# A five-layer-step graph network on one core: the late scatters go from a straight line of 196 into a loop that first copies each round

## The reference

```python
h = jnp.maximum(_layernorm(x, axis=-1), 0.0)
x = x + _L0_gnn_ref(...)   # relu(segment_sum(h[src] @ w[edge_type], dst) + h @ w_loop + b)
h = jnp.maximum(_layernorm(x, axis=-1), 0.0)
x = x + _L1_gnn_ref(...)   # attention with 4 heads over the edges, segment_sum over src
h = jnp.maximum(_layernorm(x, axis=-1), 0.0)
x = x + _L2_gnn_ref(...)   # two steps of: x @ W_self.T + mean_of_neighbours @ W_neigh.T + b, layer norm
h = jnp.maximum(_layernorm(x, axis=-1), 0.0)
x = x + _L3_gnn_ref(...)   # segment_sum((h @ W)[src] * norm, dst)
```

## Time and profile before

| | busy us (share of the span) | instructions |
|---|---|---|
| PE | 2799.7 (58%) | 19724 |
| DVE | 2506.3 (52%) | 11513 |
| ACT | 1947.0 (40%) | 5394 |
| POOL | 2441.8 (50%) | 2379 |

### The profile page before, as it was taken

How to read it: one execution, slowest core, us unless ns; L and a number is a source line. 1 busy time by engine, 2 the same in 40 slices (tenths; PEclk the granted TensorE clock), 3 DMA queues, 4 the chain that set the end, 5 groups by cost and what they waited for, 6 DMA issues and landing times.

```text
span 4854.1 us, 81538 instructions
## 1 busy us (share of the span) xinstructions
PE 2799.7 (58%) x19724; PEld 2445.3 (50%) x19724; DVE 2506.3 (52%) x11513; ACT 1947.0 (40%) x5394; POOL 2441.8 (50%) x2379
## 2 busy tenths in 40 slices
PE   6888877774665630067710675665128857751288
PEld 5887876654555520056610454565016646640277
DVE  5666668874555448823300784332019964430298
ACT  2222236664444421145500683232016645530187
POOL 5556635667888854455577003555740025557400
PEclk9999999997777765578855897887559978875599
DMA  4444437872333349811121783111129951111288
GB/s 153 158 156 160 158 125 240 240 220 46 41 41 41 41 101 309 278 40 38 42 64 60 238 282 113 36 35 52 55 85 321 318 162 39 37 57 55 91 278 262
DMA packets 328251, 638.77 MB, mean 132 GB/s; under 512 B 61072, under 2 KB 89776, under 8 KB 321992
## 3 DMA queue, kind: packets, MB, share of 16 engines
q1 hardware_dynamic: 233406, 501.99, 31.7%
q0 software_dynamic: 90944, 133.85, 12.5%
q10 hardware_dynamic: 3786, 1.65, 0.1%
HBM read 371.35 MB, written 277.50 MB: 134 GB/s over the span
## 4 chain that ended last, share of the span: by engine, by line
PE 18%; another core or an unknown queue 15%; issue 12%; ACT 9%; DVE 4%; SPq 3%; DMA 1%; ACTq 0%; POOL 0%; DVEq 0%; POOLq 0%
PE bank L1203 6%; ACT n_h L1035 5%; PE bank L1199 3%; PE bank L1187 2%; PE bank L1279 2%; PE bank L1169 2%; DVE out_stats L1667 1%; PE bank L1139 1%; SPq L637 1%; DMA ring<-sums 1%; ACT e_h L913 1%; DVE out_mv L1674 1%; ACT psum_out L950 1%; ACT out_sd L1074 1%
## 5 line engine op out<-in xcount | busy, mean ns | idle before, releaser
L739 POOL DMA_INDIRECT got<-rows,gidx x588 | 603.4, 1026 | 712.0 <-DMA rows<-ring 355.2
L774 POOL DMA_INDIRECT sums<-parked,last_i x588 | 570.9, 971 | 236.9 <-issue 177.9
L950 ACT ACTIVATE psum_out<-bank 128x132 f32<-128x132 f32 x784 | 219.7, 280 | 938.2 <-PE bank L1203 481.8
L1279 PE MATMUL bank<-ident,n_h 128*128 128x128 f32 x1176 | 202.6, 297 | 658.1 <-ACT n_h L1035 534.9
L1203 PE MATMUL bank<-psum_out,eq 128*128 128x132 f32 x1568 | 386.5, 331 | 237.1 <-ACT psum_out L950 133.1
L1035 ACT ACTIVATE n_h<-ring 128x128 f32<-128x128 f32 x1176 | 482.1, 482 | 73.9 <-DVE ring L1723 44.3
L1304 PE MATMUL bank<-ring,ident 128*128 128x128 f32 x2352 | 471.4, 282 | 49.6 <-issue 49.6
L1279 PEld LDWEIGHTS bank<-ident,n_h 128*128 128x128 f32 x1176 | 130.3, 146 | 717.5 <-ACT n_h L1035 583.7
L1184 PE MATMUL bank<-parked 128*128 128x128 f32 x3136 | 414.9, 286 | 32.8 <-issue 25.7
L1049 ACT ACTIVATE n_ht<-bank 128x512 f32<-128x512 f32 x294 | 175.5, 597 | 641.0 <-remote 439.0
L739 POOL DMA_INDIRECT got<-rowsg,gidx x196 | 195.6, 998 | 465.3 <-DMA rowsg<-ring 292.3
(11 more groups left out here) (182 smaller groups left out, 7201.8 us busy)
## 6 DMA issues: line engine op xcount, KB each, us to landing
ring<-sums SPq DMA_DIRECT2D x392, 264.0 KB
ring<-rows SPq DMA_DIRECT2D x392, 264.0 KB, 4.4
rows<-ring SPq DMA_DIRECT2D x294, 264.0 KB
ring<-attsums SPq DMA_DIRECT2D x98, 264.0 KB
rowsg<-ring SPq DMA_DIRECT2D x98, 264.0 KB
ring<-rowsg SPq DMA_DIRECT2D x98, 264.0 KB
sums<-parked SPq DMA_DIRECT2D x16, 1584.0 KB
attsums<-parked SPq DMA_DIRECT2D x16, 1584.0 KB
```

Source lines behind the costliest of these rows:

```text
L739: pool.indirect_dma_start(out=got[:, b, j, 0:width], out_offset=None, in_=table[:, :], in_offset=bass.IndirectOffsetOnAxis(ap=gidx[:, b, j ...
L774: pool.indirect_dma_start(out=sums[:, :], out_offset=bass.IndirectOffsetOnAxis(ap=last_i[:, t:t + 1], axis=0), in_=parked[:, t, :], in_off ...
L950: nc.scalar.activation(psum_out[:, b, j, :], bank[4 + j % 2][:, 0:W], ACT.Copy)\
L1279: last = nc.tensor.transpose(bank[b][:, k * P:(k + 1) * P], rows, ident[:, :])
```

## The change

The 196 DMAs in a line become a loop over rounds with two stages. `copy_parked(r)` waits for the round three back to have landed (`round_landed`), copies the round's row numbers from `last_i` into `sidx` and, once they are parked, its four tiles from `parked` into place r mod 4 of the gather ring `got`; the copy raises the new signal `lent`. `scatter_copied(r)`, one turn later, waits for `lent` and issues the four indirect DMAs, now from `got` and `sidx`. The rows that are written, their order and the number of DMAs are the same. The last two `round_landed` stand behind the loop.

```diff
+        lent = Signal(sem("lent"), 1)
...
-                def scatter_parked(r):
-                    pool.wait_ge(parked_ready.sem, parked_before(phase) + r + 1)
+                def copy_parked(r):
+                    b = r.mod(GOT)
+                    if r.i is not None or r.offset >= 3:
+                        round_landed(r.back(3))
+                    nc.gpsimd.tensor_copy(sidx[:, b, :], last_i[:, bass.ds(r.scaled(TPR), TPR)])
+                    pool.wait_ge(parked_ready.sem, parked_ready.after(r, parked_before(phase)))
+                    gate(pool)
+                    nc.gpsimd.tensor_copy(got[:, b, :, :], parked[:, bass.ds(r.scaled(TPR), TPR), :])\
+                        .then_inc(lent.sem, 1)
+
+                def scatter_copied(r):
+                    b = r.mod(GOT)
+                    if r.i is None and r.offset == ROUNDS - 1:
+                        round_landed(r.back(2))
+                    pool.wait_ge(lent.sem, lent.after(r, parked_before(phase)))
                     gate(pool)
                     for j in range(TPR):
-                        t = r * TPR + j
                         pool.indirect_dma_start(
-                            out=sums[:, :], out_offset=bass.IndirectOffsetOnAxis(ap=last_i[:, t:t + 1], axis=0),
-                            in_=parked[:, t, :], in_offset=None,
-                            bounds_check=bound, oob_is_err=False).then_inc(scattered[r % 2].sem, 16)
+                            out=sums[:, :], out_offset=bass.IndirectOffsetOnAxis(ap=sidx[:, b, j:j + 1], axis=0),
+                            in_=got[:, b, j, :], in_offset=None,
+                            bounds_check=bound, oob_is_err=False).then_inc(scattered[r.mod(2)].sem, 16)
...
-                    for r in range(ROUNDS + 2):
-                        if r >= 2:
-                            round_landed(r - 2)
-                        if r < ROUNDS:
-                            scatter_parked(r)
+                    run_steps(pool, [(copy_parked, 0), (scatter_copied, 1)], ROUNDS, GOT, behind=2)
+                    for r in range(ROUNDS - 2, ROUNDS):
+                        b = r % 2
+                        pool.wait_ge(scattered[b].sem, (parity_first(seg_index(phase), b) + r // 2 + 1) * 16 * TPR)
+                        pool.sem_inc(rounds_landed.sem, 1)
```

More of the change, by code:

```diff
@@ L764, in round_landed @@
                 def round_landed(r):
-                    b = r % 2
-                    pool.wait_ge(scattered[b].sem, (parity_first(seg_index(phase), b) + r // 2 + 1) * 16 * TPR)
+                    b = r.mod(2)
+                    pool.wait_ge(scattered[b].sem, scattered[b].after(r.div(2), parity_first(seg_index(phase), b)))
                     pool.sem_inc(rounds_landed.sem, 1)
-                def scatter_parked(r):
-                    pool.wait_ge(parked_ready.sem, parked_before(phase) + r + 1)
+                def copy_parked(r):
[12 more added lines that the diff above has]
+                    pool.wait_ge(lent.sem, lent.after(r, parked_before(phase)))
                     gate(pool)
                     for j in range(TPR):
-                        t = r * TPR + j
                         pool.indirect_dma_start(
-                            out=sums[:, :], out_offset=bass.IndirectOffsetOnAxis(ap=last_i[:, t:t + 1], axis=0),
-                            in_=parked[:, t, :], in_offset=None,
-                            bounds_check=bound, oob_is_err=False).then_inc(scattered[r % 2].sem, 16)
+                            out=sums[:, :], out_offset=bass.IndirectOffsetOnAxis(ap=sidx[:, b, j:j + 1], axis=0),
+                            in_=got[:, b, j, :], in_offset=None,
+                            bounds_check=bound, oob_is_err=False).then_inc(scattered[r.mod(2)].sem, 16)
                 def add_pair(r, q):
```

## The result

The changed kernel takes 4550.2 us (median of four runs, 4530.4 to 4598.3) against 4869.7 for the kernel before, a ratio of 0.937 (95% interval 0.927 to 0.946). The ratio goes by the fast runs alone; one of the four runs of the kernel before took 5860.5 us. 4580 was predicted. The profiled execution took 4543.6 us with a span of 4541.9, 312 us less than the span before.

The account below looks back on a forecast made before the run. Dense indirect DMAs were taken to make other engines late. Stages of 291 us plus 171.5 us for remaining groups made three 1387.5 instead of 1680.6, 293 us less: 4563 profiled, 4580 as median; range 4300 to 5010.

Parts of the forecast that it names:

- What bounds the kernel: Three scatter stages: dense indirect DMAs, one per 1.275 us, make instructions and signals late on engines working beside them.
- The copies' cost, +0.8 us a round: GpSimd's scatter rounds: two new copies make a round 5.9 us, a stage 291 us instead of 251.6.
- The upper bound of 7.8 us a round: GpSimd's scatter rounds if the copies' ends are exposed: 2.7 us more a round, a stage of 384 us; chance 0.06.
- 48 groups beside a stage: Node groups run during each scatter stage, at one group per round of 5.9 us; 50 of 98 remain.
- The remaining groups at 3.43 us: Node part behind each stage's scatters: 50 groups at 3.43 us each, 171.5 us.
- The catching-up behind the last scatter: After a stage's last scatter: something behind GpSimd catches up for some 24 us; it should vanish with the change.
- The edge at 1.41 us a DMA: Scatter stages: the time a scatter needs, catching-up included; the new 1.475 us lies 5% above it, so lateness should end.
- the crawl: Scatter stages before the change: other engines' slow pace beside the scatters, 24 node groups in 724 us.
- It goes wholly: Scatter stages: lateness gone, 72 groups beside, 380 a stage, 4330 us; far end of relief, whole or part 0.45.
- The crawl stays: Scatter stages: 1.475 us a DMA still too dense, 9 to 10 groups beside, 593 a stage, 4969 us; chance 0.33.

Follow-up runs that it names:

- line_idle: Changed kernel with the loop written out and the DMAs reading from `parked` and `last_i` again, the copies made but unused: 4509.1 us, ratio 0.927.
- line_narrow_2: Kernel before with its 588 scatters at 33 columns instead of 132, to another table, run again on a first-kind chip: 4854.3 us, ratio 1.000.
- same_turn: Changed kernel with the lag taken out, each round's DMAs waiting at once for its own copies, on an other-kind chip: 3749.0 us, ratio 1.025.
- loop_stale: Changed kernel without the big copy of the sums; loop, ring and small copy of row numbers stay: 4793.4 us, ratio 0.987.
- pause_add: Changed kernel with one more GpSimd addition of 128x528 a round, its result unread: 4347.9 us, ratio 0.893.
- line_narrow: Kernel before with its 588 scatters at 33 columns instead of 132, to another table, on an other-kind chip: 3647.3 us, ratio 0.998.

## Why the prediction was right, point by point

- *What bounds the kernel.* Right: the stages with the dense scatters, by lateness of signals and starts and not by work. `line_idle` shows it most plainly. The scatters' bytes as a cause are out by `line_narrow_2`.
- *The copies' cost, +0.8 us a round.* Right: 290/49 = 5.9 us a round in SAGE0, 303/49 = 6.2 in SAGE1, 281.4/49 = 5.7 in GCN. The three stages average 291.5 us, against 291 in the sum. What I did not foresee are the DMAs of up to 1.5 us beside DVE's additions, which make SAGE1's stage 12 us longer than that. They may help by thinning the stream; no run shows it.
- *The upper bound of 7.8 us a round.* Mis-sized: an exposed copy costs 0.65 us a round more (`same_turn`, on the other kind), not 2, since the 2.2 us of REL's loop are mostly SP's stores. That bound should have been read from what the row itself names as its releaser. The two gaps of that loop differ by 0.12 us, a little more than the 0.1 that was read from them; nothing hangs on it.
- *48 groups beside a stage.* The sum is right, 147 against 144; its parts are not: 57, 65 and 25. That the sum comes out is luck: too little in GCN cancels too much in the other two. GCN was taken to be like the others. Its stage stays at 1.44 us a DMA, since no addition of DVE lengthens the DMAs, but that is not enough to explain it: with 28 DMAs in 40 us SAGE0 got 8 groups done and GCN 3. The cause of the rest stays open.
- *The remaining groups at 3.43 us.* 41, 33 and 73 groups in 133, 119 and 221 us, 3.2 us each on the mean (3.25, 3.61 and 3.02): right within a tenth. The catching-up behind the last scatter, some 24 us of it in the earlier trace rows, is shorter, and that would account for the difference. In GCN TensorE takes up the next group 5.6 us after its last matmul of the stage:

```profile
4319.51 0.27 PE L1317 MATMUL bank<-ring,ident 128*128 128x128 f32 x1 [0.19 <-issue]
4325.36 1.12 PE L1292 MATMUL bank<-ident,n_h 128*128 128x128 f32 x4 [5.58 <-ACT n_h L1048]
```

- *The edge at 1.41 us a DMA.* Wrong as an edge: at 1.41 (`loop_stale`) the crawl is nearly whole. The groups beside rise steeply between 1.43 and 1.5, and the new time per DMA, 1.44 to 1.55, happens to straddle that. That the forecast hit within 1% owes something to this luck: 0.08 us a DMA less (`loop_stale`) kept a fifth of the gain, 0.3 us more (`pause_add`) made it about two thirds larger. Nor is there one edge for the whole kernel. ATT's edge part, at one DMA per 1.65 us, is not late, as the prediction read it: 616 us from its first gather to its last on the first kind (`line_narrow_2`), 611 on the other (`line_narrow`). But SAGE0's gathers, at 1.73 us on the first kind, are.
- *The rivals.* "It goes wholly" was priced at 4330 us and is what the longer pause gives, 4348. "The crawl stays" was priced at 4969; `loop_stale`, with the smallest pause, stays at 4793.
- *Not foreseen at all:* that the cause depends on the chip. The two kinds lie some 1200 us of 4855 apart. Only part of it is in the three stages (by the traces of before and `line_narrow`, 528+578+538 against 291+336+294 us from the first scatter to the last group's line 1279, 723 us). The three edge parts ahead of them hold 292 us more, as the windows above show. REL's edge part holds another 110: its gathers take 627 us on the first kind and 517 on the other (`line_narrow_2` and `line_narrow`).

**What stays open.** What it is behind GpSimd that falls behind, and where the steps of 0.70 us come from; why some chips, or some states of a chip, have it only; whether a straight line of gathers at 1.28 us crawls like the scatters there; whether evenly spread pauses work better or worse; whether a pause without work does the same; why GCN suffers more at one spacing. The runs come with a trace each, so whether the recording has a part in it is not shown either. The first kind of chip was met in three groups of runs, the other in two.

## What to carry to other kernels

When an engine's instructions start late with nothing to wait for while GpSimd issues indirect DMAs back to back, count what the other engines get done in that stretch, and try a small instruction between the DMAs whose result nobody needs: here 0.8 us more in each round of 5.1 us brought 7%, and 2 us brought 10.5%. Before crediting an edit with a gain, make its parts alone; here neither the loop nor the ring did anything, the copies did. And time the kernel before on more than one chip, since a remedy for something that only some show is a small cost (0.4%) on the others.

## What the hardware showed that I had not expected

- The same program takes some 4860 or 3655 us by the group of runs, each on its own chip; the medians of one kind agree within 0.5%. In GCN's stage GpSimd issues an indirect DMA every 1.28 to 1.29 us on both (251.1 and 253.4 us for 196); beside them the first does 7 groups of nodes and the other 83.
- The lateness does not go by the scatters' bytes: 132 or 33 columns a row give 24 and 23 groups beside the three stages.
- It can strike GpSimd itself: in `loop_stale` 81 of its 451 register instructions took 0.70 us or a multiple, against 0.06 at most in the changed kernel.
- An indirect DMA's issue of 0.97 us grows to as much as 1.5 beside a DVE instruction with two inputs in SBUF (128x512 float32): each of the 86 DMAs over 1.1 us in the changed kernel's stages overlaps one.
- On the first kind TensorE's single matmul takes 0.37 us as ever, but the next starts 2.8 us after it without a semaphore to wait for. The Trainium skill, "SBUF — State Buffer", section "SBUF: two separate sides", says that engines and DMAs cannot slow one another at the SBUF ports and TensorE waits for no one there; the matmul's own length agrees, and the late starts show that something else than these ports can still hold TensorE up beside a stream of DMAs.
